# Cross-attention and gated low-rank update: later tiles split in token order and turned by DMA, x added in the last stage, one pair of probability tiles added on GpSimd

## The chip, the cores and the metric

The kernel runs on one core of a Trainium2 chip. The metric is the device time of one execution in microseconds (us), as the median of several runs. TensorE, VectorE, ScalarE and GpSimd compute; SyncE issues nearly all DMAs, in the order in which its program lists them.

## What is computed

x is (8, 512, 1024), the context c is (8, 512, 256), all float32. There are 32 query heads and 8 key-value heads of 32 columns; each key-value head serves four query heads. Keys and values are both the context as it comes.

```python
x = x + attention(q=layernorm(x), k=c, v=c)      # softmax(q k / sqrt(32)) v, per head
# then, per token, with N = S = H = 8:
x_diff = layernorm(x)[:, None] - select_mean_diff;  x_diff /= norm(x_diff)
score  = (select_weight . x_diff) ** 2 summed over S
gate   = sigmoid(imp_slope * (score - imp_center));  scale, idx = max, argmax over N
x = x + (1 - scale) * ln + scale * (bias[idx] + degen[idx] @ (update[idx] . (ln - debias[idx])))
```

## The kernel before

**Units.** Attention goes in 64 units, one for each batch and key-value head (`UNITS`), with 16 score groups each: four key tiles `t` times four query heads `g`. A unit is cut into four quarters t = 0 to 3 in every engine's program; each engine runs its own loop over `u` and `t`, and they meet by semaphores.

**Scores in parts.** Queries and keys are float32 values split in a high and a low float16 part. `k_stack` and `q_stack` hold 97 rows: three products of parts (high by high, low by high, high by low) and a row with the negated maximum of each query (the shift). One score group (`score_keys`, L589) is four matmuls of 32 columns of keys each. ScalarE's exp (L884) takes it out of PSUM to `probs`, which holds two units.

**Row maxima.** One unit and a half ahead, `score_rows` (L551) multiplies only the high parts, queries by keys, into four PSUM banks (`s_ps`, one set), and VectorE's `largest` (L949) reduces them to `row_max`. The next quarter's product may start only when the reduction is done. When a unit's four quarters are reduced, `turn_max` (L634) transposes the maxima on TensorE, ScalarE's `make_shift` (L795) copies them once per unit, and SyncE's `send_shift` (L406) sends them by DMA to row 96 of `q_stack`, due at the next unit's score 0.

**Values and denominators.** `gather` (L603) multiplies values by probabilities, one key tile at a time, into one bank. For the denominators GpSimd adds tiles 0 and 1 of `probs` (L363) and tiles 2 and 3 (L351) into `sums`, three buffers of 2,048 columns; `first_denominators` (L616) and `last_denominators` (L626) multiply a block of ones by the two sums. VectorE transposes them (`take_denominators`, L961), inverts them (L967) and transposes the attended rows (`take_rows`, L955). GpSimd multiplies (L323) and adds x (L328) in `o_all`, to which x is loaded in 128-byte pieces (`load_addend`, L431, four to eight DMAs of 64 KB in three of four units). After each four units `store_half` (L420) stores them.

**Banks.** Scores, the transposed maxima, the denominators and the transposed tiles share three PSUM banks. A planner (L202 to L225) walks over the list `filled` in TensorE's order, gives each use the bank that is free first by the kept times in `KEPT`, and notes in `bank_before` whose release to wait for (`bank_free`, L555).

**Tiles.** 32 tiles of 128 tokens. For each, VectorE takes mean and variance, ScalarE subtracts the mean (L802) and scales (L809), TensorE transposes ten blocks in float32 (`turn_part`, L577), ScalarE copies the high part out (`high_part`, L820 and L824) and VectorE subtracts to make the low part (`low_part`, L1002 and L1008). Tiles 0 to 4 are prepared ahead of the loop, tile 5 and on one in each two units, up to unit 51. Two tiles at a time go to DRAM (`store_split`, L398 and L400) and come back by head in `load_unit` (L68 to L76).

**Last stage.** `row_moments`, `row_root`, `normalise`, `turn`, `project`, the gates, `result` and `finish` run over 32 tiles in token order, loaded from `x_attended`.

## Time and profile before

| | us |
|---|---|
| median of 3 runs (lowest, highest) | 1025.13 (1024.51, 1025.30) |
| span of the profiled execution | 1023.9 |
| first score group to last | 46.4 to 851.1 |

| engine | busy us | share |
|---|---|---|
| TensorE, matmuls | 949.4 | 93% |
| VectorE | 904.8 | 88% |
| GpSimd | 794.4 | 78% |
| ScalarE | 761.3 | 74% |

The span runs from the first to the last instruction. The ends of matmuls are modelled, so a TensorE that shows as busy may be waiting for a weight load. In the rows, PE is TensorE, PEld its weight loads, DVE VectorE, ACT ScalarE, POOL GpSimd, SPq SyncE's queue; L589 is a line of the program.

### The profile page before, as it was taken

Reading aid. Unit: us, or ns where it says so; the run is one execution under the profiler, and the core shown is the slowest. Engines: PE = TensorE matmul, PEld = TensorE weight load, DVE = VectorE, ACT = ScalarE, POOL = GpSimd, SP = SyncE. Lnnn points to the kernel's source line nnn. Section 1 sums busy time; section 2 is a strip of 40 time slices with the busy share of each in tenths; the row PEclk is TensorE's granted clock in tenths of the full one; section 3 lists DMA queues with packets and bytes.
Section 4 is the critical chain, followed back from the end, with each engine's and each line's share of the span. In section 5 each row is a group of like instructions: output and inputs, shape, how many; then the busy total and the mean of one; then the engine's idle time right before and its main releaser. Section 6 shows DMA issues by size and latency. Waiting matters only on the chain.

```text
span 1023.9 us, 24706 instructions
## 1 busy us (share of the span) xinstructions
PE 949.4 (93%) x9518; PEld 372.5 (36%) x9518; DVE 904.8 (88%) x1138; ACT 761.3 (74%) x1333; POOL 794.4 (78%) x422
## 2 busy tenths in 40 slices
PE   4789999999999999999999999999999999999996
PEld 3223233333333232333333333332222226777773
DVE  6869999999999999999999999998888876888976
ACT  7468888888888888888888888888777777554440
POOL 7158999999999999999999999998999998222110
PEclk9989999999999999999999999999999999999998
DMA  7675677767677767676767686766555744766423
GB/s 247 184 167 114 161 154 168 156 162 159 155 158 167 168 152 170 145 171 150 180 143 175 138 188 134 182 122 154 119 119 139 165 95 141 247 213 236 148 104 164
DMA packets 319876, 164.19 MB, mean 160 GB/s; under 512 B 182216, under 2 KB 307240, under 8 KB 319760
## 3 DMA queue, kind: packets, MB, share of 16 engines
q1 hardware_dynamic: 319456, 161.76, 64.3%
q8 instruction: 76, 1.25, 0.5%
q0 software_dynamic: 304, 0.85, 0.3%
q14 instruction: 40, 0.33, 0.1%
HBM read 107.58 MB, written 54.53 MB: 158 GB/s over the span
## 4 chain that ended last, share of the span: by engine, by line
PE 36%; DVE 30%; issue 25%; ACT 5%; POOL 2%; DMA 1%; SPq 0%; DVEq 0%; POOLq 0%; ACTq 0%
DVE row_max L949 14%; PE psum L589 8%; PE psum L603 6%; PE psum L616 5%; PE psum L734 5%; DVE den_t L961 4%; PE psum L551 4%; ACT probs L884 3%; PE psum L712 3%; DVE o_t L955 3%; PE psum L577 2%; DVE probs L1161 2%; DVE prod_mem L1008 2%; PE psum L700 1%; ACT prod_mem L824 1%
## 5 line engine op out<-in xcount | busy, mean ns | idle before, releaser
L884 ACT ACTIVATE probs<-psum 128x512 f32<-128x512 f32 x1024 | 554.7, 596 | 106.7 <-PE psum L589 88.7
L949 DVE TENSOR_REDUCE row_max<-psum 128x4 f32<-128x2048 f32 x248 | 566.0, 2282 | 63.5 <-PE psum L551 63.1
L589 PE MATMUL psum<-q_stack,k_stack 97*32 97x512 f16 x4096 | 335.0, 386 | 10.2 <-issue 3.6
L363 POOL TENSOR_TENSOR sums<-probs 128x2048 f32<-128x2048 f32 x63 | 287.8, 4568 | 19.5 <-ACT probs L884 19.5
L351 POOL TENSOR_TENSOR sums<-probs 128x2048 f32<-128x2048 f32 x63 | 287.2, 4558 | 10.2 <-PE psum L626 5.5
L603 PE MATMUL psum<-probs,v_in 128*32 128x512 f32 x2048 | 268.9, 598 | 1.0
L589 PEld LDWEIGHTS psum<-q_stack,k_stack 97*32 97x32 f16 x4096 | 96.8, 95 | 258.7 <-ACT probs L884 148.6
L551 PE MATMUL psum<-high_mem 32*128 32x512 f16 x992 | 98.3, 385 | 23.7 <-DVE row_max L949 20.0
L323 POOL TENSOR_TENSOR o_t<-o_t,inv 128x512 f32<-128x512 f32 x64 | 67.1, 1048 | 44.2 <-DVE inv L967 44.2
L328 POOL TENSOR_TENSOR o_all<-o_all,o_t 128x512 f32<-128x512 f32 x64 | 81.5, 1274 | 9.5 <-POOL o_t L323 0.4
L603 PEld LDWEIGHTS psum<-probs,v_in 128*32 128x32 f32 x2048 | 59.4, 111 | 61.1 <-issue 16.7
L551 PEld LDWEIGHTS psum<-high_mem 32*128 32x128 f16 x992 | 26.8, 91 | 138.3 <-DVE row_max L949 83.2
L335 POOL TENSOR_SCALAR var_eps<-mv 128x1 f32<-128x1 f32 x32 | 9.3, 290 | 82.2 <-DVE mv L1036 81.6
L626 PE MATMUL psum<-sums,ones 128*32 128x512 f32 x512 | 68.1, 604 | 0.0
L734 PE MATMUL psum<-down,probs 128*128 128x512 f32 x128 | 64.3, 632 | 3.9 <-DVE probs L1161 3.1
L616 PE MATMUL psum<-sums,ones 128*32 128x512 f32 x512 | 67.5, 597 | 0.0
L712 PE MATMUL psum<-w_all,high_mem 128*128 128x136 f32 x512 | 64.8, 280 | 1.1 <-ACT high_mem L897 1.1
L712 PEld LDWEIGHTS psum<-w_all,high_mem 128*128 128x128 f32 x512 | 62.2, 191 | 5.2 <-issue 4.1
L577 PE MATMUL psum<-ident,xa 128*128 128x128 f32 x256 | 45.3, 310 | 16.0 <-ACT xa L809 10.5
L824 ACT ACTIVATE prod_mem<-psum 128x512 f16<-128x512 f32 x60 | 35.8, 597 | 32.0 <-PE psum L577 32.0
L897 ACT ACTIVATE high_mem<-psum 128x1024 f32<-128x1024 f32 x32 | 32.4, 1013 | 29.5 <-PE psum L700 29.5
L955 DVE STREAM_TRANSPOSE o_t<-psum 128x512 f32<-128x512 f32 x64 | 44.3, 692 | 8.2 <-PE psum L603 4.3
(120 smaller groups left out, 788.9 us busy)
## 6 DMA issues: line engine op xcount, KB each, us to landing
q_stack<-q_split SPq DMA_DIRECT2D x192, 128.0 KB, 3.4
xa<-in_x_dram SPq DMA_DIRECT2D x32, 512.0 KB, 4.7
o_all<-in_x_dram SPq DMA_DIRECT2D x256, 64.0 KB, 2.5
x_attended<-o_all SPq DMA_DIRECT2D x64, 256.0 KB, 4.1
out_dram<-probs SPq DMA_DIRECT2D x32, 512.0 KB, 2.9
q_split<-prod_mem SPq DMA_DIRECT2D x15, 1024.0 KB, 5.4
xa<-x_attended SPq DMA_DIRECT2D x16, 512.0 KB, 4.5
probs<-x_attended SPq DMA_DIRECT2D x16, 512.0 KB, 5.3
```

The source lines that it names most:

```text
L328: pool.tensor_tensor(o_all[:, half, :, h, :], o_all[:, half, :, h, :], turned_rows, ALU.add).then_inc(o_made, 1)
L351: pool.tensor_tensor(sums[:, (2 * u - 1) % SUMS], probs[:, (u - 1) % 2, 2], probs[:, (u - 1) % 2, 3], ALU.add).then_inc(back_done, 1)
L363: pool.tensor_tensor(sums[:, 2 * u % SUMS], probs[:, u % 2, 0], probs[:, u % 2, 1], ALU.add).then_inc(front_done, 1)
L551: last = pe.matmul(s_ps[:, g, :], q_high[rows, u % SLOTS, t * P:(t + 1) * P], k_high[rows, u % SLOTS, :], start=True, stop=True)
L589: last = pe.matmul(st_ps[row:row + D, bank_of["score", u, n], :], k_stack[:, u % SLOTS, t * P + row:t * P + row + D], q_stack[:, u % SLOTS ...
L603: last = pe.matmul(o_ps[g * D:(g + 1) * D, :], v_in[:, u % 2, t, :], probs[:, u % 2, t, g, :], start=(t == 0), stop=(t == ST - 1))
L616: pe.matmul(st_ps[g * D:(g + 1) * D, bank_of["den", u, 0], :], ones[:, 0:D], sums[:, 2 * u % SUMS, g, :], start=True, stop=False)
L712: last = pe.matmul(z_ps[:, t % 2, 0:WC], yT[:, t % 2, c, :], w_all[:, c, :], start=(c == 0), stop=(c == EC - 1))
L734: last = pe.matmul(result_bank(n)[:, half * 512:(half + 1) * 512], mixT[:, t, :], down[:, half * 512:(half + 1) * 512], start=True, stop=True)
L884: act.activation(probs[:, s, keys, g, :], st_ps[:, bank_of["score", u, n], :], ACT.Exp, scale=EXP_SCALE).then_inc(exped, 1)
L949: dve.reduce_max(row_max[:, u % 2, t:G * ST:ST], s_ps[:], AX.X).then_inc(reduced, 1)
L955: dve.transpose(o_t[:, u % 2, :], o_ps[:]).then_inc(o_taken, 1)
```

## The change

From tile 5 on the split is made in token order: ScalarE makes the high parts of context (`split_context`) and normalised x (`high_part`) in float16, GpSimd the low parts (`low_parts`), and one transposing DMA for the context (`turn_c`) and one for x (`turn_x`) bring both parts to the layout that is stored. Normalising is one ScalarE pass, scale and bias together, for which GpSimd makes the bias after each inverse root. Six tiles are loaded up front.

x is no longer loaded to `o_all`; GpSimd writes the scaled rows there with one instruction. Each tile of x is loaded whole beside its attended tile and added by GpSimd (`add_x`) in the last stage, eight of them in the last units of the loop.

GpSimd adds tiles 0 and 1 of a unit's probabilities only. TensorE multiplies ones by tile 2, by that sum and by tile 3, in the next unit's quarters 0 and 1. VectorE takes the denominators in quarter 1. Gathers of tiles 0, 1 and 2 stand in quarters 2, 3 and 3; the maxima are transposed ahead of the product of quarter 2. `sums` has two buffers. SyncE's order is new. The last unit's denominators are still made of two sums, on VectorE.

```diff
-            BEGIN = ((0, 4, 9, 13, NSC), (0, 4, 8, 12, NSC))
-            MIDST = ((2, 6, 11, 15), (2, 6, 10, 14))
-            CENTRE_AT = (13, NSC)
+            C_SPLIT_AT, CENTRE_AT, HIGH_AT, SHIFT_AT = 4, 6, 2, 8
...
 
             filled = [("part", n, i) for n in range(FIRST) for i in range(PIECES)]
             for u in range(-AHEAD, UNITS + 2):
                 for t in range(ST):
-                    scores = [("score", u, n) for n in range(BEGIN[u % 2][t], BEGIN[u % 2][t + 1])] if live(u) else []
-                    half = MIDST[u % 2][t] - BEGIN[u % 2][t]
-                    if u % 2 == 1 and t < PIECES and whole(tile_of(u)):
-                        filled.append(("part", tile_of(u), t))
-                    filled += scores[:half]
                     if t == 2 and live(u + 1):
                         filled.append(("max", u + 1, 0))
-                    filled += scores[half:]
-                    if t == (ST - 1 if u % 2 == 1 else 2) and live(u - 1):
+                    if t == 0 and live(u - 1):
                         filled.append(("den", u - 1, 0))
-            KEPT = {"score": 2, "max": 2, "den": (5, 5), "part": 6}
+                    if live(u):
+                        filled += [("score", u, n) for n in range(G * t, G * (t + 1))]
+            KEPT = {"score": 2, "max": 2, "den": 9, "part": 2}
...
-                if use[0] == "part" and use[1] >= FIRST and use[2] > 0:
-                    bank = bank_of["part", use[1], use[2] - 1]
                 bank_of[use] = bank
                 if last_in[bank] is not None:
                     bank_before[use] = last_in[bank]
-                kept = KEPT["den"][use[1] % 2] if use[0] == "den" else KEPT[use[0]]
-                free_at[bank], last_in[bank] = max(i, free_at[bank]) + kept + 1, use
+                free_at[bank], last_in[bank] = max(i, free_at[bank]) + KEPT[use[0]] + 1, use
...
+                def low_parts(n):
+
+                    pool.wait_ge(c_high, n - FIRST + 1)
+                    pool.tensor_scalar(c_tile(n), c_tile(n), UP, None, ALU.mult).then_inc(c_scaled, 1)
+                    turned(pool, n - 2, "c")
+                    pool.wait_ge(c_scaled, 2 * (n - FIRST) + 1)
+                    pool.tensor_tensor(c_parts(n)[:, 1], c_tile(n), c_parts(n)[:, 0], ALU.subtract
+                                       ).then_inc(c_scaled, 1)
+                    turned(pool, n - 2, "x")
+                    pool.wait_ge(x_high, n - FIRST + 1)
+                    pool.tensor_tensor(x_parts(n)[:, 1], x_tile(n), x_parts(n)[:, 0], ALU.subtract
+                                       ).then_inc(low_done, 1)
...
+                    if h == 0:
+                        wait(pool, a_out[half], 64 * (u // KV))
+                    pool.tensor_tensor(o_all[:, half, :, h, :], o_t[:, u % 2].rearrange("p (a d) -> p a d", d=D),
                                        inv[:, u % 2].unsqueeze(2).to_broadcast([P, S // D, D]),
-                                       ALU.mult).then_inc(o_scaled, 1)
-                    wait(pool, xo_in[half], 16 * G * HALF * (u // KV + 1))
-                    wait(pool, o_scaled, u + 1)
-                    pool.tensor_tensor(o_all[:, half, :, h, :], o_all[:, half, :, h, :], turned_rows,
-                                       ALU.add).then_inc(o_made, 1)
+                                       ALU.mult).then_inc(o_made, 1)
+
+                def add_x(n):
+
+                    q, k, t = n // ST, n // ST % GROUPS, n % ST
+                    pool.wait_ge(t_in[ST * k + t], 16 * (q // GROUPS + 1))
+                    if n < EARLY * ST:
+                        pool.wait_ge(add_in[n % 2], 16 * (n // 2 + 1))
+                    else:
+                        pool.wait_ge(add_in[2 + (n - EARLY * ST) % 3], 16 * ((n - EARLY * ST) // 3 + 1))
+                    attended = xa[k][:, t].rearrange("p (g h d) -> p g h d", g=G, h=KV)
+                    pool.tensor_tensor(attended, attended, x_addend(n).rearrange("p (h g d) -> p g h d", h=KV, g=G),
+                                       ALU.add).then_inc(added, 1)
...
+                for u in range(-AHEAD, UNITS + 1):
+                    if u % 2 == 0 and whole(tile_of(u)) and u > -AHEAD:
+                        inverse_root(tile_of(u))
+                    if u % 2 == 1 and whole(tile_of(u)):
+                        low_parts(tile_of(u))
...
-                    if live(u - 2):
-                        normalise(u - 2)
-                    if u % 2 == 1 and whole(tile_of(u) + 1):
-                        inverse_root(tile_of(u) + 1)
                     if 0 <= u < UNITS - 1:
                         wait(pool, exped, NSC * u + NSC // 2)
                         wait(pool, den_done, u - 1)
-                        pool.tensor_tensor(sums[:, 2 * u % SUMS], probs[:, u % 2, 0], probs[:, u % 2, 1],
+                        pool.tensor_tensor(sums[:, u % SUMS], probs[:, u % 2, 0], probs[:, u % 2, 1],
                                            ALU.add).then_inc(front_done, 1)
+                    if u == UNITS:
+                        add_x(EARLY * ST - 1)
+                        row_root(1, 1, 0)
+                        row_root(1, 1, 1)
+                    if live(u - 1):
+                        normalise(u - 1)
+                    if 0 <= u - 1 - (UNITS - KV) < EARLY * ST - 1:
+                        add_x(u - 1 - (UNITS - KV))
 
                 for n in range(ST + 2, TILES):
+                    if n + 2 < TILES:
+                        add_x(n + 2)
...
+                def turn_x(n):
+
+                    sp.wait_ge(low_done, n - FIRST + 1)
+                    if n % 2 == 0:
+                        sp.wait_ge(split_out, stored(n // 2))
+                    sp.dma_start_transpose(q_parts_of(n)[:, :, :, n % 2 * P:(n % 2 + 1) * P]
+                                           .rearrange("p l h s -> p (l h) s"),
+                                           x_parts(n).rearrange("p l e -> p (l e)")).then_inc(turned_in["x"][n % 2], 16)
...
-                for u in range(-AHEAD, UNITS + 2):
+                for n in range(UPFRONT + 2, UPFRONT + FIRST):
+                    load_x(n)
+
+                for u in range(-AHEAD, UNITS):
                     n = tile_of(u)
-                    if u % 2 == 0 and (n - 1) % 2 == 1 and FIRST <= n - 1 < TILES:
-                        store_split(n - 1)
                     if SLOTS <= u + 3 < UNITS:
                         wait(sp, scored, NSC * u)
                         if (u + 3) % KV == 0:
...
                     if live(u) and live(u + 1):
                         load_v(u + 1)
+                    if u % 2 == 1 and whole(n):
+                        turn_c(n)
+                    if u % 2 == 0 and (n - 1) % 2 == 1 and whole(n - 1):
+                        store_split(n - 1)
+                    if live(u - 2) and (u - 2) % HALF == HALF - 1:
+                        store_half(u - 2)
+                    if u % 2 == 0 and n + UPFRONT - 1 < TILES and u > -AHEAD:
+                        load_x(n + UPFRONT - 1)
+                    if live(u) and live(u + 1):
                         send_shift(u + 1)
-                    if live(u - 3) and (u - 3) % HALF == HALF - 1:
-                        store_half(u - 3)
-                    if live(u + 1):
-                        for g in ((1,), (2, 3), (), (0,))[u % HALF]:
-                            load_addend((u + 1) // HALF, g)
-                    if live(u) and u % 2 == 0 and n + 2 < TILES:
-                        load_x(n + 2)
+                    if u % 2 == 1 and whole(n):
+                        turn_x(n)
...
                     if UNITS - KV <= u < UNITS:
                         n = u - (UNITS - KV)
                         sp.dma_start(xa_early[n // ST][:, n % ST, :], a_tiles[n]).then_inc(t_in[n], 16)
+                        load_addend(n)
...
+                def denominators(u, i):
+
+                    if i == 0:
+                        bank_free("den", u, 0)
+                    terms = (probs[:, u % 2, 2], sums[:, u % SUMS], probs[:, u % 2, 3])[i]
+                    if i == 1:
+                        pe.wait_ge(front_done, u + 1)
                     else:
-                        pe.wait_ge(front_done, u + 1)
-                    bank_free("den", u, 0)
-                    wait(pe, den_taken, u)
-                    for g in range(G):
-                        pe.matmul(st_ps[g * D:(g + 1) * D, bank_of["den", u, 0], :], ones[:, 0:D],
-                                  sums[:, 2 * u % SUMS, g, :], start=True, stop=False)
-
-                def last_denominators(u):
-
-                    if u == UNITS - 1:
-                        pe.wait_ge(last_sums, 2)
-                    else:
-                        pe.wait_ge(back_done, u + 1)
+                        pe.wait_ge(exped, NSC * u + (G * 3, 0, NSC)[i])
                     for g in range(G):
                         last = pe.matmul(st_ps[g * D:(g + 1) * D, bank_of["den", u, 0], :], ones[:, 0:D],
-                                         sums[:, (2 * u + 1) % SUMS, g, :], start=False, stop=True)
+                                         terms[:, g, :], start=(i == 0), stop=(i == 2))
+                    if i == 2:
+                        last.then_inc(den_done, 1)
...
-                for u in range(-AHEAD, UNITS + 2):
+                for u in range(-AHEAD, UNITS + 1):
                     for t in range(ST):
-                        if u == -1 and t == 2:
-                            turn_max(0)
+                        if t == 2 and live(u + 1):
+                            turn_max(u + 1)
                         if 0 <= maxima_at(u, t)[0] < HALVED:
                             first_rows(*maxima_at(u, t))
                         elif live(maxima_at(u, t)[0]):
                             score_rows(*maxima_at(u, t))
-                        if t == ST - 1 and live(u - 1) and live(u) and u % 2 == 0:
-                            last_denominators(u - 1)
-                        if t == 0 and live(u - 2) and u % 2 == 0 and u < UNITS:
-                            last_denominators(u - 2)
-                        if u % 2 == 1 and t < PIECES and whole(tile_of(u)):
-                            turn_part(tile_of(u), t)
...
+                        if t == 0 and live(u - 1) and live(u):
+                            denominators(u - 1, 0)
+                        if t == 1 and live(u - 1) and live(u):
+                            denominators(u - 1, 1)
+                        if t == ST - 1 and live(u):
+                            gather(u, 1)
                         if live(u):
-                            score_keys(u, BEGIN[u % 2][t], MIDST[u % 2][t])
-                        if u == UNITS - 1:
-                            score_keys(u, MIDST[u % 2][t], BEGIN[u % 2][t + 1])
-                        if t == 0:
-                            if live(u - 1):
-                                gather(u - 1, ST - 1)
-                        elif live(u):
-                            gather(u, t - 1)
-                        if t == 2 and 0 < u + 1 < UNITS:
-                            turn_max(u + 1)
-                        if 0 <= u < UNITS - 1:
-                            score_keys(u, MIDST[u % 2][t], BEGIN[u % 2][t + 1])
-                        if t == (ST - 1 if u % 2 == 1 else 2) and live(u - 1) and live(u):
-                            first_denominators(u - 1)
-                        if u == UNITS - 1 and t == ST - 1:
-                            last_denominators(u - 1)
+                            score_keys(u, G * t, G * t + 2)
+                        if t == 0 and live(u - 1):
+                            gather(u - 1, ST - 1)
+                        if t == 1 and live(u - 1) and live(u):
+                            denominators(u - 1, 2)
+                        if t == 2 and live(u):
+                            gather(u, 0)
+                        if t == ST - 1 and live(u):
+                            gather(u, 2)
+                        if live(u):
+                            score_keys(u, G * t + 2, G * (t + 1))
...
+                    for n in range(NSC):
+                        keys, g, s = n // G, n % G, u % 2
+                        if even and n == C_SPLIT_AT:
+                            split_context(tile)
+                        if even and n == CENTRE_AT:
+                            normalise_tile(tile)
+                        if odd and n == HIGH_AT:
+                            high_part(tile)
+                        if n == SHIFT_AT and live(u + 1):
                             make_shift(u + 1)
+                        if g == 0:
+                            wait(act, pv_done, ST * (u - 2) + keys + 1)
+                            if keys < ST // 2:
+                                wait(act, front_done, u - 1)
+                            else:
+                                wait(act, den_done, u - 1)
...
+                        wait(act, scored, NSC * u + n + 1)
+                        act.activation(probs[:, s, keys, g, :], st_ps[:, bank_of["score", u, n], :], ACT.Exp,
+                                       scale=EXP_SCALE).then_inc(exped, 1)
...
                         if t == 0 and live(u - 1):
                             take_rows(u - 1)
-                        if t == 1 and live(u - 2):
-                            invert(u - 2)
-                        if early and t == 0 and u == 0:
-                            first_moments(n + 1)
-                        if early and t == 1:
-                            last_moments(n + 1)
-                        if early and t == 2:
-                            variance(n + 1)
-                            guard(n + 1)
-                        if live(u) and u % 2 == 1 and t == ST - 1 and whole(tile_of(u + 1) + 1):
-                            first_moments(tile_of(u + 1) + 1)
-                        if t == ST - 1 and live(u - 1) and live(u) and u % 2 == 0:
+                        if t == 1 and live(u - 1) and live(u):
                             take_denominators(u - 1)
+                        if t == 2 and live(u - 1) and live(u):
+                            invert(u - 1)
+                        if u % 2 == 0 and t == 3 and whole(n):
+                            first_moments(n)
+                        if u % 2 == 1 and t == 2 and whole(n):
+                            last_moments(n)
+                        if u % 2 == 1 and t == 3 and whole(n):
+                            variance(n)
+                            guard(n)
```

## Rows read from the trace of the kernel before

**Rows 1.** Busy time of PE, PEld, DVE, ACT, POOL by stretch; clock, DMA share, GB/s.
```profile
400.00:600.00 200.00, 192.50 (x2118) 60.70 (x2119) 186.83 (x175) 168.50 (x309) 184.49 (x72) 1.00 0.71 159
900.00:920.00 20.00, 19.48 (x124) 15.31 (x123) 17.94 (x56) 10.02 (x12) 4.46 (x12) 1.00 0.61 211
```

**Rows 2.** Timeline of ACT, the shift copies: start, us, engine, line, operation, tiles, count, idle before.
```profile
402.90 0.27 ACT L795 ACTIVATE shift<-psum 16x128 f16<-16x128 f32 x1
...
428.21 0.27 ACT L795 ACTIVATE shift<-psum 16x128 f16<-16x128 f32 x1
...
718.92 0.27 ACT L795 ACTIVATE shift<-psum 16x128 f16<-16x128 f32 x1 [0.18 <-PE psum L634]
...
743.04 0.27 ACT L795 ACTIVATE shift<-psum 16x128 f16<-16x128 f32 x1 [0.18 <-PE psum L634]
```

**Rows 3.** Timeline of PE alone, 414 to 420 us.
```profile
414.81 0.28 PE L634 MATMUL psum<-ident,row_max 128*16 128x128 f32 x1
415.02 0.62 PE L589 MATMUL psum<-q_stack,k_stack 97*32 97x512 f16 x8
...
416.49 0.39 PE L551 MATMUL psum<-high_mem 32*128 32x512 f16 x4
416.81 1.07 PE L626 MATMUL psum<-sums,ones 128*32 128x512 f32 x8
417.69 0.62 PE L589 MATMUL psum<-q_stack,k_stack 97*32 97x512 f16 x8
418.13 1.04 PE L603 MATMUL psum<-probs,v_in 128*32 128x512 f32 x8
418.99 0.40 PE L589 MATMUL psum<-q_stack,k_stack 97*32 97x512 f16 x4
419.32 0.39 PE L551 MATMUL psum<-high_mem 32*128 32x512 f16 x4
```

**Rows 4.** Timeline of all engines, 744 to 763 us.
```profile
744.40 0.40 PE L551 MATMUL psum<-high_mem 32*128 32x512 f16 x4
...
744.85 2.29 DVE L949 TENSOR_REDUCE row_max<-psum 128x4 f32<-128x2048 f32 x1 [1.05 <-PE psum L551]
...
745.61 0.62 PE L589 MATMUL psum<-q_stack,k_stack 97*32 97x512 f16 x8
...
746.05 1.08 ACT L884 ACTIVATE probs<-psum 128x512 f32<-128x512 f32 x2 [1.58 <-PE psum L589]
...
747.06 0.71 DVE L961 STREAM_TRANSPOSE den_t<-psum 128x512 f32<-128x512 f32 x1
...
747.24 0.39 PE L551 MATMUL psum<-high_mem 32*128 32x512 f16 x4
...
761.49 0.71 DVE L961 STREAM_TRANSPOSE den_t<-psum 128x512 f32<-128x512 f32 x1
...
762.36 0.62 PE L589 MATMUL psum<-q_stack,k_stack 97*32 97x512 f16 x8
```

**Rows 5.** Groups by line, shapes apart: busy us, mean ns of one, idle before.
```profile
L363 POOL TENSOR_TENSOR sums<-probs 128x2048 f32<-128x2048 f32 x63 | 287.8, 4568 | 19.5 <-ACT probs L884 19.5
...
L1008 DVE SCALAR_TENSOR_TENSOR prod_mem<-psum,prod_mem 128x512 f16<-128x512 f32 x60 | 40.7, 679 | 3.1 <-ACT prod_mem L824 3.1
...
L802 ACT ACTIVATE xa<-xa,neg_mean 128x1024 f32<-128x1024 f32 x32 | 36.8, 1150 | 0.8 <-DVE var_eps L994 0.8
```

**Rows 6.** Timeline of all engines, the first units.
```profile
63.12 0.38 ACT L820 ACTIVATE k_parts<-psum 128x256 f16<-128x256 f32 x1 [3.43 <-DMA k_split<-k_parts]
...
63.56 1.05 PE L589 MATMUL psum<-q_stack,k_stack 97*32 97x512 f16 x8 [3.64 <-issue]
```

**Rows 7.** DMA queues, and an issue group with its median us to landing.
```profile
q1 hardware_dynamic: 319456, 161.76, 64.3%
...
q_stack<-shift SPq DMA_DIRECT2D x64, 4.0 KB, 2.1
```

**Rows 8.** Timeline of SyncE's queue, a unit's loads from the first to v's.
```profile
434.14 0.49 SPq L68 DMA_DIRECT2D high_mem<-q_split  x1
...
438.13 0.42 SPq L412 DMA_DIRECT2D v_in<-in_ctx_dram  x1
```

## What the change was predicted to do

> **What bounds the kernel now.** I read the busy time by stretches first [rows 1]. Between 400 and 600 us TensorE is busy 192.5 of 200 us, VectorE 186.8, GpSimd 184.5 and ScalarE 168.5: four engines are nearly full, none is quite, and TensorE's busy time has modelled ends. Such a picture does not say which engine binds, so I went on to the beat of the loop. One shift copy (L795) is made per unit, so two of them two units apart give the period of a pair [rows 2]: 428.21 - 402.90 = 25.31 us for a pair in which a tile of the next batch is prepared, 743.04 - 718.92 = 24.12 us for a pair without one (from unit 53 on). Then I followed one stretch in order of time, TensorE alone and with its partners [rows 3, 4]. The reader should see a ring there: a four-way product for the row maxima starts (744.40), VectorE's reduction of it starts 0.45 us later (744.85) and takes 2.29, and the next such product can start only about 0.1 us after that (747.24). With nothing in between, a round lasts 2.8 us, so a unit's four rounds cannot take less than 11.3 us. The unit takes 12.06 (24.12 / 2), so VectorE's ring, together with the places where TensorE comes late to it, is the bound. GpSimd's two big additions are 4.57 us each [rows 5] but nobody stands long behind them; ScalarE is not full.
>
> **What TensorE's steps cost.** From the starts in [rows 3]: a maxima product of four, 0.32 us (416.49 to 416.81); a pair of score groups, 0.44 (417.69 to 418.13); a gather step, 0.86 to 0.87 (418.13 to 418.99); a denominator step, 0.88 (416.81 to 417.69); the maxima's transpose, 0.21 (414.81 to 415.02). One score group followed by a maxima product takes 0.33 (418.99 to 419.32) where half a pair is 0.22: the turn from one shape to the other costs 0.11.
>
> **Part by part, what leaves.** For 27 tiles, tile 5 on, the ten fp32 transposes on TensorE, the second normalising pass and the third copy on ScalarE (one pass over 1,024 columns is 1.15 us [rows 5]), and three subtractions on VectorE. This lies in 26 of the pairs and is the whole difference of 25.31 - 24.12 = 1.2 us a pair. GpSimd loses one addition of 4.57 us a unit and the addition of x. It is not the bound, so that is worth nothing by itself, and its new work (an 0.5 us pass and two subtractions for a tile, together about 3.5 us each second unit, estimated from 2,048 elements in 4.57 us) fits into the 4.57 us that it gives up.
>
> **What arrives.** Denominators now take three steps on TensorE a unit instead of two: +0.88 us. More important is where they stand. The new list fills them at quarters 0 and 1, and marks their PSUM bank as kept for nine uses. Worked through with the new list and kept times, the planner gives the denominators' bank next to score group 6 of the same unit, while groups 0 to 5 share the other two. Group 6 must wait for `den_taken`. VectorE takes the denominators in quarter 1 only after that quarter's reduction. Behind group 6, on TensorE's in-order queue, stand group 7, the maxima's transpose and the maxima product of quarter 2, for which VectorE is then idle.
>
> Now one unit, product to product of the maxima, each segment being the later of the ring and TensorE's work:
>
> Quarter 1 to 2: product to reduction 0.45; reduction 2.29 less 0.08 overlap (744.85 to 747.06); transposing the denominators 0.71; release to score 0.16 (761.49 + 0.71 = 762.20, score at 762.36) [rows 4]. Group 6 starts 3.53 us after the product. Then scores 6 and 7, 0.44, turn 0.11, maxima's transpose 0.21: 4.29.
>
> Quarter 2 to 3: 2.80, the bare ring; TensorE's own work (0.32, two score pairs, one gather, two short waits for exps) is a little under it.
>
> Quarter 3 to 0: TensorE has 0.32 + 0.87 + 0.44 + 0.87 + 0.44 + 0.11 = 3.05.
>
> Quarter 0 to 1: 0.32 + 0.88 + 0.44 + 0.87 + 0.44 + 0.11 = 3.06, and a wait of about 0.1 at score 3: with two banks left it must wait for exp 1; a score reaches ScalarE 0.44 us after its start (745.61 to 746.05) and two exps take 1.08 [rows 4], by which score 3 starts 1.6 us after score 0 where it could after 1.53. Sum 3.16.
>
> The unit: 4.29 + 2.80 + 3.05 + 3.16 = 13.3, against 12.06. A pair without a tile: 26.6, that is +2.5. In a pair with a tile, ScalarE's high part (1.15 us) comes before exp 2 of the odd unit and pushes score 5, the second denominator step and their transpose by about 0.4; the second half of the moments lies behind quarter 2's reduction and costs about 0.1. ScalarE's other two new passes come while it waits for scores 4 and 6 and are hidden by that wait; if it were gone they would cost up to 1.5 us a pair. So 27.1, that is +1.8.
>
> **The sum.** 26 pairs x 1.8 = +47; 5.5 pairs x 2.5 = +14. Early in the loop TensorE stands for 3.7 us behind a ScalarE copy that waited for the store of the split [rows 6]; that wait moves to SyncE's queue: -4. Ahead of the loop ScalarE and VectorE lose a tile's passes between the first maxima: on VectorE alone some five passes of the kind of 0.68 us [rows 5], 3.4 us. I take -4, between 0 (three inverse roots now stand behind GpSimd's clearing of constants and may hold tile 3 back by as much) and -7 (ScalarE's passes add in full). In the last stage GpSimd adds x: 24 times about 2.3 us, against 4.5 us of GpSimd work in 20 us [rows 1]; hidden except where two inverse roots come close together, 0 to 2.3 us a batch, taken as +2 in all. Together +55. Span 1023.9 plus 1.2 around it is the median, 1025.1; so 1080 us.
>
> Bounds of the walk: without the turns and the exp wait a unit is 12.87, giving 26 x 0.9 + 5.5 x 1.6 - 6 = +26, 1051; with ScalarE's high pass exposed in full (1.15 for 0.4) and 0.1 more a unit for the transpose's turn, (0.75 + 0.2) x 31 = +29 more, 1109.
>
> **What the DMA transposes cost.** No row shows one. A tile and its context make 5,120 pieces of 128 bytes, if it moves so. All packets of the main queue took 64.3% of 16 engines' time for 319,456 packets [rows 7], 0.033 us each, so 5,120 would take 10.6 us of all sixteen, in a pair of 27. The loads of x in 128-byte pieces that go away were 4,096 a pair. So the traffic is about even. On SyncE's queue a shift needs 2.1 us to land [rows 7]; it is due at score 0 of the next unit. In a fourth of the units it now stands behind the unit's eight loads (434.14 to 438.55 us [rows 8]), v, the store of a split, and the next x. I count 9 to 12 us from the unit's start, where the shift is made at about 8, and find it still 1 to 3 us early. Turning x is issued behind the shift, so it has some 12 us.
>
> By the Trainium skill, *VectorE: DVE Perf Modes*, The three transpose paths, a 128x128 block of two-byte values takes the DMA path 1309 ns; sixteen in a row for x would be an estimated 21 us, which would speak against this change. *Advanced Engine Details and Errata*, X-Bar Transpose, also in the Trainium skill, says instead that such DMAs are as fast as regular ones, by which x would cost no more than a store of the same size. No row of the trace before decides.
>
> **Rivals.** (A) The wait for the bank is covered, and the ring runs free: the segment of quarters 1 to 2 is then 2.9, reduction and transpose back to back (744.85 to 747.77 [rows 4]). A unit is 11.9, a pair with a tile 24.3, without 23.8: 26 x -1.0 + 5.5 x -0.3 - 6 = -34, 991 us. It decides once segment 1 to 2 is over 0.9 us shorter than I say. For it: all four engines lose or keep work except TensorE. Against: the planner's bank and the order of the queue leave no other way. Chance 0.12.
>
> (B) The transposes or SyncE's queue come late for the shift. Where the x transpose takes double (two packets a piece, 21 us by the packet price above), shifts land some 8 us late in each pair, less 1 of slack: 26 x 7 = +180 on top, 1262. The mild form, 3 us late once in four units, 13 times, is +39, 1119. Against: slack of 1 to 3 us and even traffic. Chance 0.14, most of it mild.
>
> (C) TensorE's added step fits into its present waits and the gains at the start cancel the rest: within 2 us of 1025. It needs the low bound and more. Chance 0.03.
>
> The forecast has 0.71. Range 1040 to 1120: it takes the walk's bounds and the mildest of B, and leaves out A and the rest of B. A measurement here can tell about 0.2%, 2 us. Faster 0.12, same 0.03, slower 0.85.
>
> **What would show it.** Per-unit shift copies 13.3 us apart in late units; TensorE's score line waiting for the transpose of the denominators some 60 times, about 1 us each; VectorE idle before the reduction of quarter 2; GpSimd down to some 60% busy. If score groups never wait for that transpose, my walk is wrong (A). If the score line waits on the shift's DMA, it is B.

## The result, and the profile after

The changed kernel takes 1128.61 us (median of 4 runs, 1126.83 to 1131.13), the kernel before 1024.82 beside it (4 runs, 1022.09 to 1025.30). The ratio is 1.1017, 95% interval 1.0995 to 1.1039. Slower was forecast, but by 55 us; it is 104. The range ended at 1120.

The page of the changed kernel, profiled at 1125.7 us; first busy time by engine, then the span in 40 slices of 28 us (tenths busy; PEclk is the granted clock in tenths).

```profile
span 1125.7 us, 24731 instructions
PE 969.1 (86%) x9752; PEld 365.8 (32%) x9752; DVE 906.9 (81%) x1025; ACT 715.0 (64%) x1274; POOL 608.7 (54%) x440
...
PE   4659999999889989999999989989999985889797
...
PEclk9979999999999999999999999999999997999999
```

GpSimd fell from 78% to 54% of the span and TensorE from 93% to 86%. TensorE is busy 20 us more in all and VectorE 2, against a span that is 102 us longer: most of the time is not added work, the work stands further apart. Two places show in the slices: the third, and the last seven, of which only two still have a 9.

I cut both spans at the shift copies (one for each unit, as in [rows 2]). This gives the most useful table of the case, in us:

| stretch | before | after | difference | forecast |
|---|---|---|---|---|
| start to first shift copy | 40.9 | 40.3 | -0.6 | -4 |
| first to third shift copy | 32.6 | 41.8 | +9.1 | -4 |
| third to last shift copy | 765.8 | 822.9 | +57 | +61 |
| last shift copy to end | 184.6 | 220.7 | +36 | +2 |
| span | 1023.9 | 1125.7 | +102 | +55 |

**The loop is as forecast.** The last units of the changed kernel, its shift copies:

```profile
730.69 0.25 ACT L860 ACTIVATE shift<-psum 16x128 f16<-16x128 f32 x1
744.09 0.25 ACT L860 ACTIVATE shift<-psum 16x128 f16<-16x128 f32 x1
```

That is 13.40 us where the walk had 13.3 and [rows 2] 12.06; pairs with a tile are 13.40 + 13.57 = 26.97 where it had 27.1. One unit of TensorE alone, from the product of quarter 1 on:

```profile
806.29 0.39 PE L620 MATMUL psum<-high_mem 32*128 32x512 f16 x4
...
807.93 1.04 PE L686 MATMUL psum<-probs,ones 128*32 128x512 f32 x8
809.81 0.62 PE L658 MATMUL psum<-q_stack,k_stack 97*32 97x512 f16 x8 [0.84 <-DVE den_t L1021]
810.36 0.28 PE L705 MATMUL psum<-ident,row_max 128*16 128x128 f32 x1
810.57 0.39 PE L620 MATMUL psum<-high_mem 32*128 32x512 f16 x4
...
813.43 0.39 PE L620 MATMUL psum<-high_mem 32*128 32x512 f16 x4 [0.34 <-DVE row_max L1009]
...
816.48 0.39 PE L620 MATMUL psum<-high_mem 32*128 32x512 f16 x4
...
819.68 0.39 PE L620 MATMUL psum<-high_mem 32*128 32x512 f16 x4
```

The reader should see score groups 6 and 7 (809.81) wait for VectorE's transpose of the denominators, with the maxima's transpose and the product of quarter 2 queued behind them. The four segments are 4.28, 2.86, 3.05 and 3.20 us; forecast were 4.29, 2.80, 3.05 and 3.16. VectorE's side of the same wait, and then the sum of such waits over the whole span (columns are us in total, times, longest; PEld is TensorE's weight load):

```profile
809.04 0.72 DVE L1021 STREAM_TRANSPOSE den_t<-psum 128x512 f32<-128x512 f32 x1
811.08 2.29 DVE L1009 TENSOR_REDUCE row_max<-psum 128x4 f32<-128x2048 f32 x1 [1.33 <-PE psum L620]
```
```profile
PEld psum L658 <- DVE den_t L1021: 110.4, 63, 1.8
...
ACT prod_mem L910 <- POOL neg_mr L382: 81.0, 25, 13.8
```

VectorE, the ring of [rows 4], idles 1.33 us ahead of the reduction of quarter 2. The second line belongs to the last stage: ScalarE waits 81 us for GpSimd's roots.

**The start stops longer.** SyncE's queue and TensorE around unit 1:

```profile
57.08 4.92 SPq L428 DMA_TRANSPOSE prod_mem<-xa  x1
...
64.38 0.38 SPq L458 DMA_DIRECT2D q_split<-prod_mem  x1
...
69.28 0.59 SPq L466 DMA_DIRECT2D q_stack<-shift  x1
```
```profile
73.33 1.04 PE L658 MATMUL psum<-q_stack,k_stack 97*32 97x512 f16 x8 [12.27 <-issue]
```

The shift of unit 1 is copied at 52.98 us, and the DMA that carries it goes out at 69.28. Ahead of it on the queue stand tile 5's turns and the store that waits for them. TensorE stands 12.27 us where it stood 3.64 in [rows 6]. The same shift was already late in the kernel before: copied at 55.77 us, it went out behind the store of a split, which is these two rows of SyncE's queue there:

```profile
57.36 2.55 SPq L400 DMA_DIRECT2D k_split<-k_parts  x1
...
61.13 0.89 SPq L406 DMA_DIRECT2D q_stack<-shift  x1
```

**The last stage is slower throughout.** Windows of 20 us (busy us of PE, PEld, DVE, ACT, POOL, then granted clock, DMA share, GB/s), the changed kernel first and then the one before:

```profile
940.00:960.00 20.00, 7.55 (x40) 6.98 (x39) 7.48 (x21) 5.01 (x6) 9.28 (x10) 0.66 0.69 239
960.00:980.00 20.00, 17.25 (x91) 12.01 (x91) 17.23 (x42) 7.14 (x8) 11.03 (x14) 0.91 0.63 222
```
```profile
960.00:980.00 20.00, 19.48 (x119) 14.89 (x118) 17.52 (x54) 9.32 (x10) 4.75 (x14) 1.00 0.29 120
```

First there is a hole (7.55 of 20 us), then TensorE makes 91 to 116 matmuls in each of the next four windows, where it made 119 before. The hole, on GpSimd and SyncE:

```profile
947.63 2.34 POOL L369 TENSOR_TENSOR probs<-probs 128x1024 f32<-128x1024 f32 x1 [11.26 <-DMA probs<-in_x_dram]
```
```profile
936.46 3.38 SPq L480 DMA_DIRECT2D x_attended<-o_all  x4
...
941.29 1.19 SPq L494 DMA_DIRECT2D probs<-in_x_dram  x1
```

The load of x for tile 8 is listed behind the store of the last unit; its addition begins after GpSimd has stood 11.26 us for it, and the roots are queued behind.

### The profile page after: what moved, and what is told of

Same layout as the page of the kernel before. It is cut to its first block, busy times and chain, and to the rows that moved or that the text cites. A ratio compares the mean times of both kernels' runs of the same rounds, so it can differ in the third digit from the quotient of the medians.

```text
span 1125.7 us, 24731 instructions
## 1 busy us (share of the span) xinstructions
PE 969.1 (86%) x9752; PEld 365.8 (32%) x9752; DVE 906.9 (81%) x1025; ACT 715.0 (64%) x1274; POOL 608.7 (54%) x440
## 4 chain that ended last, share of the span: by engine, by line
PE 65%; DVE 23%; DMA 4%; issue 3%; POOL 2%; SPq 1%; ACT 1%; DVEq 0%; POOLq 0%; ACTq 0%
PE psum L658 17%; PE psum L686 16%; PE psum L672 16%; DVE row_max L1009 12%; PE psum L620 8%; DVE den_t L1021 4%; PE psum L800 3%; DMA probs<-in_x_dram 3%; PE psum L778 2%; DVE probs L1212 2%; PE psum L705 1%; PE psum L766 1%; POOL probs L369 1%; DMA ctx_mem<-in_ctx_dram 1%; DVE row_max L1000 1%
## 5 line engine op out<-in xcount | busy, mean ns | idle before, releaser
L396 POOL TENSOR_TENSOR sums<-probs 128x2048 f32<-128x2048 f32 x63 | 287.5, 4563 | 320.2 <-ACT probs L948 320.2
L686 PE MATMUL psum<-probs,ones 128*32 128x512 f32 x1008 | 132.5, 598 | 0.0
L300 POOL TENSOR_TENSOR xa<-xa 128x1024 f16<-128x1024 f32 x27 | 57.8, 2141 | 58.4 <-ACT xa L894 58.4
L672 PEld LDWEIGHTS psum<-probs,v_in 128*32 128x32 f32 x2048 | 60.7, 109 | 40.5 <-ACT probs L948 16.1
L356 POOL TENSOR_TENSOR o_all<-o_t,inv 128x512 f32<-128x512 f32 x64 | 68.0, 1063 | 0.0
L686 PE MATMUL psum<-sums,ones 128*32 128x512 f32 x504 | 67.2, 605 | 0.0
L369 POOL TENSOR_TENSOR probs<-probs 128x1024 f32<-128x1024 f32 x16 | 37.8, 2360 | 40.3 <-DMA probs<-in_x_dram 40.3
L1021 DVE STREAM_TRANSPOSE den_t<-psum 128x512 f32<-128x512 f32 x64 | 45.9, 717 | 7.1 <-PE psum L686 5.2
L766 PE MATMUL psum<-ident,prod_mem 128*128 128x128 f32 x256 | 36.0, 287 | 12.6 <-ACT prod_mem L910 12.5
L887 ACT ACTIVATE xa<-xa,neg_mean,rstd 128x1024 f32<-128x1024 f32 x32 | 39.7, 1240 | 10.8 <-POOL neg_mean L287 10.8
L910 ACT ACTIVATE prod_mem<-xa,neg_mr,rstd 128x1024 f32<-128x1024 f32 x16 | 19.7, 1240 | 41.5 <-POOL neg_mr L382 41.5
```

Of the source, the lines that this page charges most:

```text
L300: pool.tensor_tensor(x_parts(n)[:, 1], x_tile(n), x_parts(n)[:, 0], ALU.subtract).then_inc(low_done, 1)
L356: pool.tensor_tensor(o_all[:, half, :, h, :], o_t[:, u % 2].rearrange("p (a d) -> p a d", d=D), inv[:, u % 2].unsqueeze(2).to_broadcast([P ...
L396: pool.tensor_tensor(sums[:, u % SUMS], probs[:, u % 2, 0], probs[:, u % 2, 1], ALU.add).then_inc(front_done, 1)
L672: last = pe.matmul(o_ps[g * D:(g + 1) * D, :], v_in[:, u % 2, t, :], probs[:, u % 2, t, g, :], start=(t == 0), stop=(t == ST - 1))
L686: last = pe.matmul(st_ps[g * D:(g + 1) * D, bank_of["den", u, 0], :], ones[:, 0:D], terms[:, g, :], start=(i == 0), stop=(i == 2))
L1021: dve.transpose(den_t[:], st_ps[:, bank_of["den", u, 0], :]).then_inc(den_taken, 1)
```

## Experiments

The kernel before took 1021.6 to 1021.9 us beside e1 to e8, which are one run each, and 1021.76 beside f1 to f3 and e9, which have four. "Stage" is the time from the last shift copy to the end: before 184.6, after 220.7.

**The bank.** The planner was told that the denominators' bank is kept for eleven uses, so that group 6 gets another bank.

```diff
-            KEPT = {"score": 2, "max": 2, "den": 9, "part": 2}
+            KEPT = {"score": 2, "max": 2, "den": 11, "part": 2}
```

> The planner's kept time for the denominators' bank is 11 instead of 9: score groups 6 and 7 use the other two banks and the maxima's transpose gets that bank. Theory W (the wait for the denominators' bank at group 6 stretches the unit): groups 6 and 7 and the turn, 0.5 us, now run under that wait, so a late unit falls from 13.40 to about 12.9 us and the time by 62 x 0.5 = 31 us, to about 1097. Rival P (TensorE's added work by itself makes the unit long, the wait is only where its slack lies): unit 13.40, time within 3 us of 1128.

Measured 1100.94 us, late units 12.94, most pairs with a tile 13.80 + 12.24 = 26.04. P had the same time as the changed kernel and falls.

**Bank and order.** The same, and the product of quarter 2 ahead of the maxima's transpose:

```diff
-                        if t == 2 and live(u + 1):
-                            turn_max(u + 1)
                         if 0 <= maxima_at(u, t)[0] < HALVED:
...
                             score_rows(*maxima_at(u, t))
+                        if t == 2 and live(u + 1):
+                            turn_max(u + 1)
```

> As the run with kept time 11, and in quarter 2 the maxima product stands ahead of the maxima's transpose, so that nothing between the products of quarters 1 and 2 waits for the denominators. Theory W: that segment is 3.1 us (TensorE's own work) instead of 4.3; a unit is about 12.3 us, the time 62 x 1.1 = 68 us less, about 1060. Rival P: the unit stays over 13 us, since TensorE's work in it is the same.

Measured 1078.27 us. Shift copies of late units:

```profile
794.60 0.27 ACT L860 ACTIVATE shift<-psum 16x128 f16<-16x128 f32 x1
806.91 0.27 ACT L860 ACTIVATE shift<-psum 16x128 f16<-16x128 f32 x1
```

12.31 us, as the walk said. The time is 18 us above what was expected. The 1060 takes 1.1 us off each of 62 units, but pairs with a tile go to 25.2, 1.8 off and not 2.2 (26 x 0.4 = 10); and some units are longer than the usual ones, six of them 13.6 to 15.2 us, 11 us in all. SyncE, ScalarE and TensorE in one of these:

```profile
231.82 3.64 SPq L480 DMA_DIRECT2D x_attended<-o_all  x4
235.50 1.38 SPq L466 DMA_DIRECT2D q_stack<-shift  x1
```
```profile
232.59 0.27 ACT L860 ACTIVATE shift<-psum 16x128 f16<-16x128 f32 x1
```
```profile
241.00 0.61 PE L658 MATMUL psum<-q_stack,k_stack 97*32 97x512 f16 x8 [1.98 <-issue]
```

The shift is ready at 232.86 and leaves after the store, at 235.50. In the changed kernel this order is the same, and its longer units hide nearly all of it (1.3 us in all above the usual ones): rival B in its mild form stands behind the forecast mechanism and appears once that is mended.

**Steps left out.** The denominators' step for tile 2 left out, and in another kernel that for tile 3:

```diff
+                    if i == 0:
+                        return
...
```

> Leaves out the first denominator step on TensorE (tile 2, in quarter 0): the denominators lack tile 2. Theory W: the segment from quarter 0 to 1 falls from 3.2 us to the ring's floor of 2.8, so 0.4 us a unit and 25 us in all, about 1103. Rival P: each unit is 0.88 us shorter, 55 us in all, about 1073.

Measured 1106.75 us, late units 13.00: 0.40 less each, as said, and pairs of 26.0. Twelve units are 13.5 to 14.2 us long, about 9 us in all; in the one that I followed, TensorE waits 1.37 us for the DMA of the shift, which stood behind a store as in bank and order.

```diff
+                    if i == 2:
+                        return
...
```

> Leaves out the last denominator step on TensorE (tile 3, in quarter 1): the denominators lack tile 3. Theory W: nothing, because group 6 waits for quarter 1's reduction and the transpose of the denominators behind it, which do not move: 1125 to 1129. Rival P: 0.88 us a unit, 55 us in all, about 1073.

Measured 1133.86 us, 5 above the range of W and 60 above P's. Units stay at 13.4, as said, but every third or fourth is 14.3. The windows of the run without the step, then of the changed kernel:

```profile
400.00:600.00 200.00, 172.81 (x1890) 50.93 (x1882) 166.51 (x132) 145.25 (x270) 115.36 (x68) 0.96 0.63 151
```
```profile
400.00:600.00 200.00, 180.17 (x2019) 52.64 (x2019) 168.24 (x134) 145.80 (x273) 115.36 (x65) 1.00 0.67 151
```

With less work TensorE's granted clock is 0.96 here, where it is 1.00 with it: part of the time it ran at 1.2 GHz in place of 2.4. In a long unit it is 0.90. TensorE waits 1.52 us for the denominators' bank there, where it is 0.84 in the changed kernel, and the matmuls behind that wait take nearly twice their time. A gather there, and one 3 us later:

```profile
274.34 1.92 PE L672 MATMUL psum<-probs,v_in 128*32 128x512 f32 x8
...
277.06 1.07 PE L672 MATMUL psum<-probs,v_in 128*32 128x512 f32 x8
```

What is shown is that the clock fell in a kernel whose only edit gave TensorE longer idle stretches, and that the long units go with it. The busy time over 200 us doesn't decide this: without tile 2's step it is 173.3 us, about the same, at a granted clock of 1.00.

**x in the last stage.** Loads and additions of x left out altogether:

```diff
-                    pool.tensor_tensor(attended, attended, x_addend(n)...
+                    pool.memset(spot[:, n % 2:n % 2 + 1], 0.0).then_inc(added, 1)
...
```

> Leaves x out of the last stage: neither its loads nor GpSimd's additions, only a one-column store in their place, so the result lacks x. Theory X (the last stage is long because GpSimd's additions wait for x): from the last shift copy to the end 220.7 us become about 185, as before the change, and the time falls by 33 to 36 us, to about 1094. Rival Q (the rest of the stage suffers from something else, as the lower granted clock of 0.88 to 0.95 there): less than half of it, 1112 or more.

Measured 1090.62 us, stage 183.1, against 184.6 before. All of the +36 is x. In this kernel nothing is otherwise undone: its loop is the changed kernel's. Q falls.

**The start.** Unit 1's shift sent ahead of tile 5's turns and store:

```diff
-                    if u % 2 == 1 and whole(n):
+                    if u > 0 and u % 2 == 1 and whole(n):
                         turn_c(n)
...
+                    if u == 0:
+                        turn_c(n - 1)
+                        turn_x(n - 1)
+                        store_split(n - 1)
```

> SyncE sends the shift of unit 1 before it issues the transposes of tile 5 and the store of its pair, instead of after them. Theory S (that shift, sent at 69.3 us though made at 53, is the whole stop at unit 1): the third distance between shift copies falls from 29.1 us to about 16, the time by 12 to 13 us, to about 1116. Rival: the stop moves to the next thing that stands behind the store of the split, and the time falls by less than 5 us.

Measured 1122.84 us; the distance of 29.1 us (the second) is 20.42. SyncE reaches the shift at 57.50 only, for it has the loads of units 2 and 3 and of four tiles to issue first. TensorE still stands 4.28 us there, in place of 12.27, and it stood 3.64 in the kernel before. So the shift's place was the cause of what was new; my expectation of 12 to 13 us took the old stop with it and was too high. The distance fell by 8.7 us and the time by 5.8: the last stage, whose code is the same, was 3.2 us longer in this one run.

**Which part of x.** The loads for tiles 8 to 10 put at unit 62, and in a second kernel each step's load of x ahead of its store and load as well:

```diff
                             load(EARLY, EARLY, t)
+                        for t in range(3):
+                            load_addend(EARLY * ST + t)
                 store_half(UNITS - 1)
...
```

> The first three x tiles of the late set (8 to 10) are loaded as soon as unit 62 is done, ahead of the last unit's store, instead of behind it. Theory X1 (half a stage's loss is that these loads are issued at 941 us although their memory is free at 914): the stop of 12.4 us on TensorE at 940 to 952 us goes, and the time falls by about 12 us, to 1116. Rival: the later tiles set the pace anyway and under 5 us are won.

> As the run with early loads, and within the last stage each load of x is issued ahead of the store and the load of its step, so that it waits only for its own slot and not for a finished tile. Theory X2 (x's loads stand behind waits for finished tiles on SyncE's queue): another 20 us or so go, TensorE is busy 19 of 20 us as before, the time is about 1096. Rival Y (three slots are too few, or GpSimd is late by itself): as the run with early loads, within 4 us.

Measured 1119.24 us (stage 211.8) and 1118.09 us (209.5). The hole goes, as X1 said, though the time fell by 9 us and not 12. X2 is refuted: the second edit gave 1 us, not 20, which is what Y had. 25 us above 184.6 stay, and TensorE is busy 16.4 to 17.4 of 20 us between 960 and 1040 us. I looked at VectorE beside GpSimd in the second kernel:

```profile
1031.29 0.19 DVE L1173 TENSOR_TENSOR upd_sb<-upd_sb,cst 128x32 f32<-128x32 f32 x1
1031.49 2.35 POOL L369 TENSOR_TENSOR probs<-probs 128x1024 f32<-128x1024 f32 x1 [1.54 <-DMA probs<-in_x_dram]
1031.51 2.37 DVE L1174 TENSOR_TENSOR upd_sb<-upd_sb,neg_slope 128x32 f32<-128x32 f32 x1
...
1035.25 2.36 POOL L369 TENSOR_TENSOR probs<-probs 128x1024 f32<-128x1024 f32 x1
1035.58 2.07 DVE L1183 TENSOR_SCALAR upd_sb<-z_e 128x32 f32<-128x32 f32 x1
```

An operation on 32 columns that takes 0.19 us lasts 2.37, and ends (1033.88) 0.04 us after GpSimd's addition (1033.84). So I had three theories: the gates' instructions wait for GpSimd (P), the roots stand behind the additions in GpSimd's queue (Q), or the DMA traffic grew too much (D).

**Loads without additions** (from tile 8 on):

```diff
+                    if n >= EARLY * ST:
+                        pool.memset(spot[:, n % 2:n % 2 + 1], 0.0).then_inc(added, 1)
+                        return
...
```

> Base is e8_x_first (1118.1 us, last shift copy to end 209.5). All loads of x stay, but from tile 8 on GpSimd's addition of x is left out (a memset of one column takes its place), so x of those tiles is missing from the output. Three theories on what holds the rest of the last stage. D, DMA traffic: the loads of x (a third more bytes in the stage) are what is left; the stage stays at 205 to 210, time 1115 to 1118. Q, GpSimd's queue: the inverse roots stand behind additions of 2.36 us. P, VectorE: its small instructions of the gates that read and write only SBUF (the product with the negated slope: 987 ns in e8_x_first, 192 in the kernel before) end 0.02 to 0.04 us after one of GpSimd's additions, as if they waited for it; added over the gates' lines that is 3.0 us a batch, 24 us in eight batches. By Q or P the stage goes back to 184 to 187, time 1093 to 1096, and by P the product with the negated slope is back at 0.19 us.

Measured 1094.43 us, stage 186.2; a window of it:

```profile
1000.00:1020.00 20.00, 19.48 (x119) 14.83 (x119) 17.85 (x58) 9.43 (x10) 4.57 (x16) 1.00 0.91 330
```

The DMAs move 330 GB/s, and TensorE makes its 119 matmuls again. D falls, and the additions are 23.3 us of the stage (209.5 - 186.2). VectorE's product with the negated slope is back at 0.19 us, which P asked for.

**Roots first, five places for x:**

```diff
                 for n in range(ST + 2, TILES):
+                    row_root(n // ST, n // ST % GROUPS, n % ST)
                     if n + 2 < TILES:
                         add_x(n + 2)
-                    row_root(n // ST, n // ST % GROUPS, n % ST)
...
```

> Base e8_x_first. x tiles of the last stage get five places in place of three, and GpSimd makes the inverse root of tile n ahead of the addition for tile n + 2, not behind it. Theory Q: ScalarE's 33.9 us of waiting for the roots mostly goes, and the stage shortens by 15 to 20, time 1098 to 1103. Theory P: the gates' small instructions are still as long as GpSimd's additions wherever they meet (sum over their lines still about 3 us a batch), so the stage gains 2 to 5 at most, time 1113 to 1116. Theory D: no change, 1118.

Measured 1117.22 us, stage 209.4. Q falls: ScalarE's waits for the roots shrank, from 33.9 to 21.4 us, and the stage did not. Nor did it gain by two more places for x. P had 1113 to 1116, a little too much.

**Additions after the gates:**

```diff
...
+                for b in range(EARLY, B):
+                    pool.wait_ge(mix_done, b - 1)
+                    add_x(ST * b)
+                    for t in range(ST - 1):
+                        add_x(ST * b + t + 1)
+                        root(ST * b + t)
+                    root(ST * b + ST - 1)
```

> As f2_root_first, but GpSimd makes a batch's four additions only when VectorE has finished the gates of the batch two before (a wait for the mix), so that no addition lies beside the gates. Theory P: the gates' small instructions are back at 0.15 to 0.2 us each and the stage is 15 to 24 us shorter than in f2_root_first, time 1092 to 1100. Theory Q: additions in a bunch put roots later again, so 0 to 10 us longer than f2_root_first. Theory D: no change.

Measured 1103.31 us, stage 194.6. The same instruction of the gates (groups by line; busy us, mean ns of one, idle before), in e8, in roots first, in this kernel, and in the kernel before:

```profile
L1174 DVE TENSOR_TENSOR upd_sb<-upd_sb,neg_slope 128x32 f32<-128x32 f32 x8 | 7.9, 987 | 0.3
```
```profile
L1177 DVE TENSOR_TENSOR upd_sb<-upd_sb,neg_slope 128x32 f32<-128x32 f32 x8 | 5.8, 727 | 0.3
```
```profile
L1183 DVE TENSOR_TENSOR upd_sb<-upd_sb,neg_slope 128x32 f32<-128x32 f32 x8 | 1.5, 192 | 0.3
```
```profile
L1121 DVE TENSOR_TENSOR upd_sb<-upd_sb,neg_slope 128x32 f32<-128x32 f32 x8 | 1.5, 192 | 0.3
```

The additions are the same number and about as long; what has changed is when they run. The gates' 184 instructions of VectorE together take 62.5 us of the stage in roots first, 41.5 in this kernel and 41.6 in the kernel before. P holds: 21 us of VectorE's time were waiting for GpSimd, in instructions that show as busy. But the stage is only 14.8 us shorter (P had 15 to 24), because the new order makes a new wait. VectorE's statistics of a tile now wait for its addition (us in total, times, longest):

```profile
DVE stats L1104 <- POOL probs L370: 11.1, 16, 2.5
...
DVE stats L1104 <- POOL xa L370: 5.0, 8, 0.9
```

That is 16.1 us, against 1.3 in roots first.

**The transpose of x issued twice:**

```diff
+                    sp.dma_start_transpose(q_parts_of(n)[:, :, :, n % 2 * P:(n % 2 + 1) * P]
...
+                    sp.wait_ge(turned_in["x"][n % 2], 32 * ((n - FIRST) // 2) + 16)
```

> Base is the changed kernel (1128.6 us). The transposing DMA of x is issued a second time, behind the first one's end, for each of the 27 tiles. My walk (W): the transposes are hidden, since the shift stands ahead of them; late units have none, units with a tile stay at 27.0 a pair, time 1127 to 1131. Rival B (the transposes are late): SyncE's queue is held some 7 us longer in each pair with a tile, the store or a shift comes late, and pairs grow by 1 us or more, time 1150 or above.

Measured 1168.26 us. W was wrong here and B right. Late units stay at 13.40 and many pairs at 26.97, but others are up to 32.5, and the start is 4.8 us longer. SyncE's queue in one stretch:

```profile
459.13 3.00 SPq L428 DMA_TRANSPOSE prod_mem<-xa  x1
463.86 1.86 SPq L432 DMA_TRANSPOSE prod_mem<-xa  x1
465.77 1.06 SPq L68 DMA_DIRECT2D high_mem<-q_split  x1
...
476.06 1.16 SPq L470 DMA_DIRECT2D q_stack<-shift  x1
```

In the changed kernel, with one transpose, pairs stay at 26.97, so one is hidden. The second issue and the wait for the first hold the queue some 3 to 4 us longer (in the changed kernel the loads of the next unit go out 466.72 - 463.66 = 3.1 us after the transpose's start, here 465.77 - 459.13 = 6.6), and the shifts behind the store of a split or of attended rows come late. So SyncE has less than that to spare; the 12 us that I gave the transpose hold for its landing and not for its place in the queue. The edit adds a wait and a transfer at once, and doesn't tell these apart.

**All mended at once:** bank and order, the start, early loads, five places, additions after the gates, and each shift sent right behind its unit's loads:

```diff
+                    if live(u) and live(u + 1):
+                        send_shift(u + 1)
                     if u > 0 and u % 2 == 1 and whole(n):
                         turn_c(n)
```

> All mendings in one kernel: the denominators' bank kept for eleven uses, the maxima's transpose behind the product of quarter 2, the additions of x after the gates with five places and early loads, no transposes or store ahead of the second shift, and SyncE sends each shift directly behind its unit's loads. If the causes found are the whole of it and add up: late units 12.32 (e2_order), pairs with a tile 25.2 without the long ones, so 26 x -0.1 and 5.5 x +0.5 against the kernel before, the first two distances 33 as before, the last stage 194.6 as in f3_after_gates (+10), together span 1032 to 1034, time 1035. If the long units of e2_order have another cause than SyncE's order, they stay, 1045 to 1052. If something of the change's 104 us is still unnamed, it is over 1050 with none of the named rows in sight.

Measured 1044.20 us (5 runs; the kernel before 1024.3 beside them; ratio 1.0194, interval 1.0173 to 1.0215). The loop from first to last shift copy is 807.4 us (before 798.4, after 864.7) and the stage 193.6. Late units are 12.32 and pairs with a tile 25.18.

It is 9 us above what I expected, and most of that is long units. From the fourth distance on they are together 8 us above the usual ones, where e2_order has 11. Only two are over 13.6 us (13.65 and 15.64) and not six, but the longest alone is 3.5 us too long. SyncE's queue ahead of it:

```profile
590.37 4.71 SPq L435 DMA_TRANSPOSE prod_mem<-xa  x1
...
600.39 0.59 SPq L473 DMA_DIRECT2D q_stack<-shift  x1
```

The shift is copied at 596.55 and leaves at 600.39. It no longer stands behind the store, but behind its unit's loads, and these behind the transpose and the store. So the new order moved the lateness of the shift and did not take it away; that SyncE's order is the cause stands on such rows, and no run here takes it away. The second and third distances are 18.2 each, since unit 4's loads now wait for the store of tile 5; with the first, 11.0, that is 1 to 2 us more than expected. The change's 104 us are reduced to 20, and no version here beats the kernel before.

## Why the prediction was half right

**The bound and the ring** [rows 1 to 4]: right. Reading the ring of maxima products in order of time gave each segment to 0.06 us.

**The bank at group 6**: right, and shown by taking it away: e1_kept and e2_order gave the unit times that the same walk gives. Rival A needed the wait to be covered; 63 waits say it is not. A denominators' step costs 0.40 of its 0.88 us in quarter 0, where the ring's 2.80 is reached without it (e5_no_den0), and nothing in quarter 1, where the wait for the bank ends last (e6_no_den2, in its units at full clock). The 12.32 against 12.06 that is left with bank and order mended may be the third step; no run tests it.

**Pairs with a tile**: 27.1 against 26.97, right.

**The start** (-4 forecast, +9.1 measured): a step failed, not a size. I wrote that the wait for the split's store "moves to SyncE's queue" and counted that as a gain. On SyncE it holds everything listed behind it, and one of these is a shift, due at the next unit's first score. I had applied this very test to steady units and not to the first. The reading of [rows 6] was incomplete as well: ScalarE's copy ended at 63.50 us and the score started at 63.56, but the shift, sent at 61.13, landed at an estimated 63.2, by the 2.1 us of [rows 7]. Taking away the wait of the copy alone could have won some 0.3 us and not 3.7.

**Ahead of the loop** (-4, -0.6): the passes taken from VectorE and ScalarE were not on the path. No run tells why.

**The last stage** (+2, +36): the largest error, in the step "hidden except where two inverse roots come close together". I costed GpSimd's 24 additions of 2.3 us against GpSimd's own free time [rows 1], and found 4.5 of 20 us busy. The duration was right (2.36) and the free time too. Missing were two other partners: VectorE, whose instructions wait for an addition that runs beside them, and SyncE's queue, on which the loads of x stand late:

| part of the stage | us | from |
|---|---|---|
| loads of x listed late on SyncE | 11.2 | 220.7 - 209.5, after and e8 |
| additions of x from tile 8 on | 23.3 | 209.5 - 186.2, e8 and f1 |
| the first eight additions, and all loads with their traffic | 3.1 | 186.2 - 183.1, f1 and e3 |

Six kernels that differ from the changed one only ahead of this stage had stages of 216.4 to 223.9 us (e1, e2, e4 to e6, e9), so the first two rows are good to about 4 us, and the last is no more than such a difference. The 23.3 are matched by the gates' instructions of VectorE: these take 65.7 us in e8 and 41.6 in f1 (61.6 in the changed kernel). f3 won 14.8 of the 23.3 by moving the additions. The 8.4 that it is still above f1 (194.6 - 186.2) need not be a part of the change's cost: f3 has 16.1 us of waits of VectorE for additions, where f1 has none, and ScalarE waits for roots 38.5 us in it. No run separates these.

**The range** ended at 1120 and the time is 1128.6. The stage is 34 us above its term and the start 13; with either of the two terms right the time would have been inside. The loop's term, 4 us too high, took a little off.

**Rival B**: not the cause of the steady loop, but real. The slack "of 1 to 3 us" fits the changed kernel's loop; e2_order and e9_turn_twice ran into it. The forecast of even traffic held: the DMA share between 400 and 600 us is 0.67, where [rows 1] has 0.71.

**The granted clock** had no term. It is 0.66 in the hole of the stage and 0.91 to 0.98 in the four windows behind it, against 1.00 before. By how much it makes these losses larger isn't separated. It is not what holds the stage: in e8 it is 1.00 from 980 to 1040 us, where TensorE is busy 16.4 to 17.4 of 20 us.

## What to carry to other kernels

Before work goes to an engine with free time, ask which other engine's instructions will run beside it and whether they can; here VectorE operations of 0.2 us waited out additions of 2.4 us on GpSimd. When a wait moves to a DMA queue, list what stands behind it on that queue, in the first units as well as in steady ones. And a bank that a planner gives by assumed keeping times has to be checked against the engine that frees it: two more uses in one table gave back 28 us.

## What was unexpected of the hardware

**VectorE waits for GpSimd.** VectorE's operations with both inputs in SBUF (0.15 to 0.19 us alone) lasted up to 2.37 us and ended 0.02 to 0.04 us behind a GpSimd addition; so did an operation of one input and a constant (L1183, 2.07 us for 0.18). Its reductions, reciprocals and statistics, and operations with one input in PSUM, kept their times: 1.65 us for four of L1214, as for the same four in f3. The Trainium skill, *SBUF — State Buffer*, Who interferes with whom, says that a VectorE instruction with two SBUF inputs contends with a GpSimd instruction that reads SBUF, that one in a two-port mode contends with GpSimd too, and that whoever issues first has the shared ports for the whole instruction while the other is blocked. The traces agree, with 2.37 for 0.19 us where the addition started 0.02 us earlier. The rule was there to be read before the forecast, and speaks against this change.

**Less work, more time.** Leaving out the denominators' step for tile 3 lowered the granted clock from 1.00 to 0.96 between 400 and 600 us, and the one run of that kernel was 5 us slower. Leaving out the one for tile 2 left the clock at 1.00, and that run was 22 us faster.

**Transposing DMAs.** The one for x, 2 parts of 128 x 1024, landed after 4.9 us in the median and held SyncE's queue for 1.7 to 4.9 us:

```profile
prod_mem<-xa SPq DMA_TRANSPOSE x27, 4.9
```

By the Trainium skill, *VectorE: DVE Perf Modes*, The three transpose paths, it would have been an estimated 21 us, sixteen blocks one after another; the trace has less than a fourth of that. *Advanced Engine Details and Errata*, X-Bar Transpose, also in the Trainium skill, which has such DMAs as fast as regular ones, is the nearer: the store of the split, twice the bytes, landed after 5.5 us. The shift's DMA landed after 3.3 us where [rows 7] has 2.1, which took part of SyncE's slack.
